# Attention stage: reciprocals spread by broadcast stationary columns, ScalarE's copies of whole turned tiles, four probability buffers

## The chip, the cores and the metric

The program runs on one core of a Trainium2 chip. The metric is the device time of one execution in microseconds (us). The engines are TensorE (PE; its weight loads are listed as PEld), VectorE (DVE), ScalarE (ACT), GpSimd (POOL) and SyncE (SP), which issues DMAs. Each engine works through its own instructions in program order; they meet only at semaphores.

## The reference, cut to what matters

The whole function is two layers of a transformer-like block (attention, a feed-forward with low-rank updates, a fake-quantised product, a mixing of streams with 50 Sinkhorn iterations). The change is in the attention of layer 0: 2 batches, 512 queries, 1024 keys, 32 heads of 32 columns, four heads sharing the keys and values of one of 8 groups.

```python
query = q @ w_q.T                      # q: layernorm(x), (2, 512, 1024)
key = k @ w_k.T                        # k, v: ctx, (2, 1024, 1024)
value = v @ w_v.T
...
scores = jnp.einsum('bghnd,bgsd->bghns', query, key) / D_HEAD ** 0.5
scores = jnp.where(mask, scores, jnp.finfo(scores.dtype).min)
attention = jax.nn.softmax(scores, axis=-1)
out = jnp.einsum('bghns,bgsd->bghnd', attention, value)
out = out.transpose(0, 3, 1, 2, 4).reshape(b, n, D_MODEL)
return out @ w_out.T
```

## The kernel before, in words

The program has five stages, one after another, each in a block of its own with a barrier behind it: `stage_a` (projections), `stage_b` (attention), `stage_c` (output projection and feed-forward), `stage_d` (quantised product), `stage_e` (streams). All is written out by hand in Bass: every engine has its own program, and semaphores order them. Only `stage_b` is touched.

`stage_b` runs over BG = 16 pairs of batch and group. One pair has STEPS = 16 steps, a step being one tile of 128 queries of one head (4 tiles of queries, 4 heads; `k % 16 = 4 * tile + head`). Two pairs make a BODY of 32 steps: the first body is written out (`first=True`), six run in a loop, the last is written out again. UNIT = 8 steps are two query tiles of all four heads.

For step k the data goes so:

1. PE scores: two matmuls (L568) of 128 queries by 512 keys into `psS[k % 2]`.
2. DVE `mask_min` (L704): adds the mask, writes `Sc[k % 4]` and each query's minimum (the scores are negated).
3. ACT `exponentials` (L652): `Pr[k % 2]` and the row sums in `sums`. It waits for `masked`, and, as the turns of step k-2 read the same buffer, for `turned[1]` of that step.
4. PE turns the 128x1024 probabilities by eight 128x128 transposes (L618) into `psT`: four into half 0, four into half 1. Each half is one PSUM bank, and there is only one of each.
5. ACT `keep` (L660) copies half 0 to `PT`, DVE `keep` (L713) copies half 1. They count `kept[0]` and `kept[1]`. PE's next turns into a half wait for its count.
6. Eight steps later PE weighs (`weigh`, L582): at each step four matmuls, one for each head, with 32 stationary columns `Vs[:, u, kt, :]` in the strip of columns of that head, 256 queries wide, summing over the eight key tiles kt into `psO`.

PE's order in step k is: scores of step k+2; first four turns of step k; the weighing; last four turns of step k. DVE's is: `mask_min` of step k+2, `keep` of step k. ACT's is: exponential of step k+1, `keep` of step k.

The normalisation is done on the output, which has its queries in columns, while the sums have theirs in partitions. For the pair before, in the steps j of the current pair: at j = 0 DVE takes the reciprocals (`rec`, L717); at j = 8 ACT copies the unnormalised output to `Os` (`keep_O`, L670); at j = 10 PE turns the reciprocals, four transposes of 128x4 (`turn_rec`, L592), at j = 12 ACT copies the result, 4x512, to `recT` (`rec_rows`, L664); at j = 13 PE multiplies it by the 0/1 matrix `headsel` (4x128), so that each head's reciprocals stand on its 32 partitions (`spread_rec`, L598); at j = 15 DVE multiplies (`normalise`, L724) and SP stores. After the last pair the same chain runs with no steps around it.

Of the kernel before, what the change touches and what calls it, by code (L numbers as in the profile page):

```python
# [30 lines left out]
P = 128  # L31
# [420 lines left out]
def stage_b(nc, mask, QHd, QLd, KHd, KLd, Vd, AOd, start_early_loads=None):  # L452
# [4 lines left out]
    with ExitStack() as stack:  # L457
        def sb(name, shape, dt=F32):
            return stack.enter_context(nc.sbuf_tensor(name, shape, dt))
# [6 lines left out]
        UNIT = 2 * HPG  # L466
        UQ = 2 * P
        assert UNIT == NK
        ident = sb("b_ident", [P, P])
        headsel = sb("b_headsel", [HPG, P])  # L470
# [6 lines left out]
        Pr = sb("b_Pr", [P, 2, S2])  # L477
# [4 lines left out]
        recT = sb("b_recT", [HPG, S])  # L482
# [8 lines left out]
        selready = sem("b_selready")  # L491
        mask_in = sem("b_mask_in")
        mbias_ready = sem("b_mbias")
        waited = sem("b_waited")
# [10 lines left out]
        rec_turned = sem("b_recturned")  # L505
        recT_ready = sem("b_recT")
        spread = sem("b_spread")
        O_kept = sem("b_Okept")
        AO_ready = sem("b_AO")
        stored = [sem(f"b_stored{u}") for u in range(2)]  # L510
        block = stack.enter_context(nc.Block())
        QKV_DMAS = 9

        def queries(k):
            return slice(k // HPG % 2 * P, (k // HPG % 2 + 1) * P)
# [43 lines left out]
        @block.tensor  # L559
        def _(pe):  # L560
            def score(it, k, very_first=False):

                u, j = divmod(k, STEPS)
                qt, h = divmod(j, HPG)
                if j == 0 and not very_first:
                    pe.wait_ge(qkv_in[u], (it + 1) * (16 * QKV_DMAS))
                for n in range(2):
                    last = pe.matmul(psS[:, k % 2, n * HALF:(n + 1) * HALF], Qs[:, u, h, qt * P:(qt + 1) * P],  # L568
                                     Ks[:, u, n * HALF:(n + 1) * HALF], start=True, stop=True)
                last.then_inc(scored, 1)  # L570

            def weigh(it, k, first=False):

                u, unit, kt = (k // UNIT - 1) // 2 % 2, k // UNIT - 1, k % UNIT
                if kt == 0:
                    pe.wait_ge(kept[0], it * BODY + k)
                    pe.wait_ge(kept[1], it * BODY + k)
                    if unit % 2 == 0 and not first:
                        pe.wait_ge(AO_ready, it * 2 + (u - 1))
                cols = slice(unit % 2 * UQ, (unit % 2 + 1) * UQ)  # L580
                for h in range(HPG):
                    last = pe.matmul(psO[h * DH:(h + 1) * DH, u, cols], Vs[:, u, kt, :], PT[:, unit % 2, kt, h, :],  # L582
                                     start=(kt == 0), stop=(kt == NK - 1))
                if kt == NK - 1:
                    last.then_inc(weighed, 1)

            def turn_rec(bg, u):

                pe.wait_ge(rec_ready, bg + 1)
                pe.wait_ge(O_kept, bg + 1)  # L590
                for qt in range(QT):
                    last = pe.transpose(psO[0:HPG, u, qt * P:(qt + 1) * P], rec[:, u, qt * HPG:(qt + 1) * HPG],  # L592
                                        ident[:])
                last.then_inc(rec_turned, 1)

            def spread_rec(bg, u):
                pe.wait_ge(recT_ready, bg + 1)
                pe.matmul(psO[:, u, :], headsel[:], recT[:], start=True, stop=True).then_inc(spread, 1)  # L598

            def body(it, first=False, last=False):  # L600
                for k in range(BODY):
                    u, j = divmod(k, STEPS)

                    if not (last and k + 2 >= BODY):
                        pe.wait_ge(masked, it * BODY + (k + 1))
                        if k + 2 < BODY:
                            score(it, k + 2)
                        else:
                            score(it + 1, k + 2 - BODY)
                    pe.wait_ge(probs, it * BODY + (k + 1))  # L610
                    for f in range(2):
                        if f == 1 and not (first and k < UNIT):
                            weigh(it, k, first)
                        if not (first and k == 0):
                            pe.wait_ge(kept[f], it * BODY + k)
                        for t in range(NK // 2):
                            kt = f * (NK // 2) + t
                            last_t = pe.transpose(psT[:, f, t, :], Pr[:, k % 2, kt * P:(kt + 1) * P], ident[:])  # L618
                        last_t.then_inc(turned[f], 1)

                    if not (first and u == 0):
                        if j == UNIT + 2:
                            turn_rec(it * 2 + (u - 1), 1 - u)
                        if j == UNIT + 5:
                            spread_rec(it * 2 + (u - 1), 1 - u)

            pe.wait_ge(setup, 2)
            pe.wait_ge(selready, 4)
# [10 lines left out]
            turn_rec(BG - 1, 1)  # L639
            spread_rec(BG - 1, 1)  # L640

        @block.scalar
        def _(act):
            def exponentials(it, k, first=False):

                act.wait_ge(masked, it * BODY + (k + 1))
                if not (first and k < 2):
                    act.wait_ge(turned[1], it * BODY + (k - 1))
                u, j = divmod(k, STEPS)
                if j == 0 and not first:  # L650
                    act.wait_ge(rec_ready, it * 2 + (u - 1))
                act.activation(Pr[:, k % 2, :], Sc[:, k % 4, :], ACT.Exp, bias=mins[:, k % 4:k % 4 + 1], scale=-1.0,  # L652
                               accum_out=sums[:, u, j:j + 1]).then_inc(probs, 1)

            def keep(it, k, first=False):
                act.wait_ge(turned[0], it * BODY + (k + 1))
                if not (first and k < 2 * UNIT):
                    if k % UNIT == 0:
                        act.wait_ge(weighed, it * (BODY // UNIT) + (k // UNIT - 1))
                act.copy(PT[:, (k // UNIT) % 2, 0:NK // 2, k % HPG, queries(k)], psT[:, 0, :, :]).then_inc(kept[0], 1)  # L660

            def rec_rows(bg, u):
                act.wait_ge(rec_turned, bg + 1)
                act.copy(recT[:], psO[0:HPG, u, :]).then_inc(recT_ready, 1)  # L664

            def keep_O(bg, u, first=False):
                act.wait_ge(weighed, (bg + 1) * (STEPS // UNIT))
# [4 lines left out]
            def body(it, first=False, last=False):  # L672
                for k in range(BODY):
# [6 lines left out]
                    if not (first and u == 0):  # L680
                        if j == UNIT:
                            keep_O(it * 2 + (u - 1), 1 - u, first and u == 1)
                        if j == UNIT + 4:
                            rec_rows(it * 2 + (u - 1), 1 - u)

            act.dma_start(mk8[:], mask.rearrange("(t p) k -> p t k", p=P)).then_inc(mask_in, 16)
            exponentials(0, 0, True)
# [2 lines left out]
                body(it)  # L690
            body(BG // 2 - 1, last=True)
            keep_O(BG - 1, 1)
            rec_rows(BG - 1, 1)

        @block.vector
        def _(dve):
# [9 lines left out]
                                         accum_out=mins[:, k % 4:k % 4 + 1]).then_inc(masked, 1)  # L706

            def keep(it, k, first=False):
                dve.wait_ge(turned[1], it * BODY + (k + 1))
                if not (first and k < 2 * UNIT):  # L710
                    if k % UNIT == 0:
# [14 lines left out]
            def body(it, first=False, last=False):  # L726
                for k in range(BODY):
# [6 lines left out]
                    if not (first and u == 0):  # L734
                        if j == 0:
                            reciprocals(it * 2 + (u - 1), 1 - u)
                        if j == UNIT + 7:
                            normalise(it * 2 + (u - 1), 1 - u, None if first else it * 16)

            dve.sem_inc(stored[1], 16)  # L740
# [15 lines left out]
        @block.gpsimd  # L756
        def _(pool):
            identity(pool, ident, setup)
            pool.memset(headsel[:], 1.0).then_inc(selready, 1)
            pool.wait_ge(selready, 1)  # L760
            pool.affine_select(out=headsel[:], in_=headsel[:], compare_op=ALU.is_ge, fill=0.0, base=0,
                               pattern=[[1, P]], channel_multiplier=-DH).then_inc(selready, 1)
            pool.wait_ge(selready, 2)
            pool.affine_select(out=headsel[:], in_=headsel[:], compare_op=ALU.is_ge, fill=0.0, base=DH - 1,
                               pattern=[[-1, P]], channel_multiplier=DH).then_inc(selready, 2)

# [1214 lines left out]
```

## Time and profile before

| | |
|---|---|
| median of 3 runs | 1275.06 us (lowest 1275.0) |
| span of the profiled execution | 1275.0 us |
| mean granted TensorE clock, whole span | 0.920 |
| PE busy | 1074.9 us (84%) |
| DVE busy | 904.2 us (71%) |
| ACT busy | 670.6 us (53%) |
| POOL busy | 131.5 us (10%) |

The span is the time from the first to the last instruction of one execution, which the profile traces; the runs are timed without it. The busy shares are means over all five stages. The attention stage's first scores start at 237 us and its last operation at 801 us, and it is in the windows and the order of events within it that the change has to be judged. A timeline row gives the start, the time for which the engine was busy with it (several instructions of a kind merged, with their number as x4), and in brackets the idle time ahead and what ended it. Successive merged rows of PE overlap at their ends, since a matmul's last columns are still on their way when the next starts; the distance of two starts is what a piece of PE's work takes.

### The profile page before, as it was taken

To read this page: it belongs to the slowest core of one execution; us is meant where nothing else is said; L and a number is where in the kernel's file an instruction comes from. 1 tells how busy PE (TensorE), PEld (TensorE's weight loads), DVE (VectorE), ACT (ScalarE), POOL (GpSimd) and SP (SyncE) were. 2 spreads that over 40 slices of the span, in tenths; PEclk is the share of its full clock that TensorE was granted. 3 is DMA by queue.
4 is the path that set the end of the run, shared out by engine and by line. 5 is a ranking of instruction groups with operands and counts; after the bars stand their busy time and mean duration, and the time that the engine had idled before them with its cause. 6 is when DMAs were issued, how large, how long until landed. Compare 5 with 4: busy or idle time off the path is not lost. (4 is left out here: it accounts for less than half of the span.)

```text
span 1275.0 us, 20748 instructions
## 1 busy us (share of the span) xinstructions
PE 1074.9 (84%) x6960; PEld 748.7 (59%) x6960; DVE 904.2 (71%) x1889; ACT 670.6 (53%) x1146; POOL 131.5 (10%) x107
## 2 busy tenths in 40 slices
PE   4999899499999999999999999689999967622208
PEld 3788777366666666666666666168888833411107
DVE  6445732598888898888888887535534336689998
ACT  3223310488888888888888887423222156543214
POOL 3111300000000000000000000000032045224300
PEclk8999999699999999999999999889999989855559
DMA  4777931952112222222222110563240000000003
GB/s 167 249 268 265 371 125 38 229 168 59 44 47 44 62 62 62 62 62 62 58 62 62 45 30 10 158 214 96 66 149 0 0 1 1 12 1 0 0 0 132
DMA packets 55719, 112.82 MB, mean 88 GB/s; under 512 B 7884, under 2 KB 21324, under 8 KB 55548
## 3 DMA queue, kind: packets, MB, share of 16 engines
q1 hardware_dynamic: 55084, 111.74, 28.6%
q8 instruction: 25, 0.41, 0.1%
q10 hardware_dynamic: 528, 0.52, 0.1%
q14 instruction: 18, 0.15, 0.0%
q0 software_dynamic: 64, 0.00, 0.0%
HBM read 83.99 MB, written 27.26 MB: 87 GB/s over the span
## 5 line engine op out<-in xcount | busy, mean ns | idle before, releaser
L652 ACT ACTIVATE b_Pr<-b_Sc,b_mins 128x1024 f32<-128x1024 f32 x256 | 294.5, 1150 | 94.8 <-PE b_psT L618 70.8
L704 DVE CUSTOM_DVE_ANT_0 b_Sc<-b_psS,b_mbias 128x1024 f32<-128x1024 f32 x256 | 312.3, 1220 | 28.5 <-PE b_psS L568 28.3
L618 PE MATMUL b_psT<-b_ident,b_Pr 128*128 128x128 f32 x2048 | 321.0, 280 | 0.9 <-ACT b_PT L660 0.2
L618 PEld LDWEIGHTS b_psT<-b_ident,b_Pr 128*128 128x128 f32 x2048 | 235.0, 141 | 140.3 <-issue 99.9
L713 DVE COPY b_PT<-b_psT 128x512 f32<-128x512 f32 x256 | 176.9, 691 | 42.6 <-PE b_psT L618 40.1
L568 PE MATMUL b_psS<-b_Ks,b_Qs 128*128 128x512 f32 x512 | 183.1, 439 | 17.5 <-DMA b_Qs<-QLd 14.4
L582 PE MATMUL b_psO<-b_PT,b_Vs 128*32 128x256 f32 x2048 | 162.2, 390 | 1.3 <-DVE b_PT L713 0.9
L660 ACT COPY b_PT<-b_psT 128x512 f32<-128x512 f32 x256 | 145.1, 567 | 13.8 <-PE b_psT L618 13.2
L568 PEld LDWEIGHTS b_psS<-b_Ks,b_Qs 128*128 128x128 f32 x512 | 78.3, 193 | 29.6 <-issue 25.2
L1039 ACT ACTIVATE c_sd<-c_mv,c_eps 128x1 f32<-128x1 f32 x16 | 4.7, 295 | 142.9 <-DVE c_mv L1121 142.9
L270 PE MATMUL a_psM<-XTh,WTh 128*128 128x512 f32 x192 | 75.7, 394 | 3.6 <-DVE WTl L345 3.6
L270 PE MATMUL a_psM<-XTh,WTl 128*128 128x512 f32 x192 | 75.2, 392 | 0.0
L270 PE MATMUL a_psM<-XTl,WTh 128*128 128x512 f32 x192 | 75.2, 392 | 0.0
L1114 DVE TENSOR_TENSOR XR<-XR,c_psM 128x1024 f32 (+1 forms) x16 | 19.5, 1221 | 75.4 <-PE c_psM L950 75.4
L582 PEld LDWEIGHTS b_psO<-b_PT,b_Vs 128*32 128x32 f32 x2048 | 42.0, 108 | 44.6 <-issue 43.7
L314 ACT ACTIVATE a_oh<-a_psM 128x512 fp32r<-128x512 f32 x24 | 14.4, 598 | 98.1 <-PE a_psM L270 91.9
L1615 PE MATMUL e_psT<-e_XN,e_dg 128*128 x128 | 30.0, 399 | 41.2 <-DVE XR L1870 41.2
L381 DVE SCALAR_TENSOR_TENSOR a_ol<-a_psM,a_oh 128x512 fp32r<-128x512 f32 x24 | 16.6, 691 | 64.9 <-ACT a_oh L314 64.9
L60 POOL MEMSET c_ident<- 128x128 f32 x1 | 0.2, 204 | 574.1 <-POOLq L457 574.1
L950 PE MATMUL c_psM<-WOh,c_Lh 128*128 128x512 f32 x128 | 51.8, 405 | 4.2 <-issue 4.2
L1615 PEld LDWEIGHTS e_psT<-e_XN,e_dg 128*128 128x128 f32 x128 | 25.7, 202 | 45.7 <-issue 41.9
L950 PE MATMUL c_psM<-WOh,c_Ll 128*128 128x512 f32 x128 | 51.8, 404 | 0.0
(219 smaller groups left out, 1673.0 us busy)
## 6 DMA issues: line engine op xcount, KB each, us to landing
a_xn<-in_ctx_turned SPq DMA_DIRECT2D x16, 512.0 KB, 3.4
XS<-in_ctx SPq DMA_DIRECT2D x16, 512.0 KB, 5.8
b_Qs<-QHd SPq DMA_DIRECT2D x30, 256.0 KB, 4.6
b_Qs<-QLd SPq DMA_DIRECT2D x30, 256.0 KB, 5.2
XS<-in_x SPq DMA_DIRECT2D x8, 512.0 KB, 10.2
a_wst<-in_L_xattn_w_q SPq DMA_DIRECT2D x8, 512.0 KB, 5.1
Q2d<-a_q SPq DMA_DIRECT2D x16, 256.0 KB, 4.7
QHd<-a_oh SPq DMA_DIRECT2D x16, 256.0 KB, 4.0
```

The lines of the kernel that those rows point to most:

```text
L270: last = pe.matmul(psM[:, slot, :], a[:, w_slot, k, :], m[:, k, cols], start=(k == 0 and a is WTh and m is mh), stop=(k == KT - 1 and a is ...
L381: dve.scalar_tensor_tensor(out=ol[:, slot, :], in0=psM[:, ps_slot, :], scalar=scale, in1=oh[:, slot, :].bitcast(F32), op0=ALU.mult, op1=AL ...
L568: last = pe.matmul(psS[:, k % 2, n * HALF:(n + 1) * HALF], Qs[:, u, h, qt * P:(qt + 1) * P], Ks[:, u, n * HALF:(n + 1) * HALF], start=True ...
L582: last = pe.matmul(psO[h * DH:(h + 1) * DH, u, cols], Vs[:, u, kt, :], PT[:, unit % 2, kt, h, :], start=(kt == 0), stop=(kt == NK - 1))
L618: last_t = pe.transpose(psT[:, f, t, :], Pr[:, k % 2, kt * P:(kt + 1) * P], ident[:])
L652: act.activation(Pr[:, k % 2, :], Sc[:, k % 4, :], ACT.Exp, bias=mins[:, k % 4:k % 4 + 1], scale=-1.0, accum_out=sums[:, u, j:j + 1]).then ...
L660: act.copy(PT[:, (k // UNIT) % 2, 0:NK // 2, k % HPG, queries(k)], psT[:, 0, :, :]).then_inc(kept[0], 1)
L704: dve.tensor_tensor_reduce(out=Sc[:, k % 4, :], in0=psS[:, k % 2, :], in1=mbias[:, qt, :], scale=1.0, scalar=3.4e38, op0=ALU.add, op1=ALU.min,
L713: dve.tensor_copy(PT[:, (k // UNIT) % 2, NK // 2:NK, k % HPG, queries(k)], psT[:, 1, :, :]).then_inc(kept[1], 1)
L950: last = pe.matmul(psM[:, u, cols], a[:, u, k, :], w[:, k, cols], start=(k == 0 and i == 0), stop=(k == KT - 1 and i == 2))
L1114: dve.tensor_tensor(row, row, psM[:, u, :], ALU.add).then_inc(added, 1)
L1615: last = pe.matmul(psX(u)[:, i * CH:(i + 1) * CH], dg[:, u, n, i, :], XN[:, ds(t, 1), n * CH:(n + 1) * CH].rearrange("p a n -> p (a n)"), ...
```

## The change

It does three things in `stage_b`, and nothing elsewhere.

`Pr` has PR = 4 buffers in place of 2. ACT's exponential of step k waits for the turns of step k-4.

In steps j = 2, 7 and 12 of each pair (`WHOLE`), ACT's `keep` copies both halves of `psT` in one instruction of 128x1024, for which it waits for `turned[1]`, and counts `kept[0]`; DVE's `keep` does nothing in these steps. `kept[1]` then counts only the other steps (`HALVED`, `halved(k)`), and PE doesn't wait for it where the step before was a whole one.

The reciprocals aren't turned. `spread_rec` (new L589) does 16 matmuls at j = 10: for each tile of queries and each head, the column of reciprocals, read 32 times over (`to_broadcast`), is the 128x32 stationary operand, and the 128x128 identity moves. The product has in all 32 partitions of the head's strip the reciprocals of the 128 queries. `turn_rec`, `rec_rows`, `headsel` and `recT` go. `normalise` moves from j = 15 to j = 13.

```diff
+        PR = 4
+        WHOLE = (2, 7, 12)
+        HALVED = BODY - 2 * len(WHOLE)
...
+        def halved(k):
+            return sum(i % STEPS not in WHOLE for i in range(k))
...
-            def turn_rec(bg, u):
+            def spread_rec(bg, u):
                 pe.wait_ge(rec_ready, bg + 1)
                 pe.wait_ge(O_kept, bg + 1)
                 for qt in range(QT):
-                    last = pe.transpose(psO[0:HPG, u, qt * P:(qt + 1) * P], rec[:, u, qt * HPG:(qt + 1) * HPG],
-                                        ident[:])
-                last.then_inc(rec_turned, 1)
-            def spread_rec(bg, u):
-                pe.wait_ge(recT_ready, bg + 1)
-                pe.matmul(psO[:, u, :], headsel[:], recT[:], start=True, stop=True).then_inc(spread, 1)
+                    for h in range(HPG):
+                        one = rec[:, u, qt * HPG + h:qt * HPG + h + 1].to_broadcast([P, DH])
+                        last = pe.matmul(psO[h * DH:(h + 1) * DH, u, qt * P:(qt + 1) * P], one, ident[:],
+                                         start=True, stop=True)
+                last.then_inc(spread, 1)
...
                     for f in range(2):
                         if f == 1 and not (first and k < UNIT):
                             weigh(it, k, first)
-                        if not (first and k == 0):
-                            pe.wait_ge(kept[f], it * BODY + k)
+                        if f == 1 and k and (k - 1) % STEPS not in WHOLE:
+                            pe.wait_ge(kept[1], it * HALVED + halved(k))
+                        elif f == 1 and k == 0 and not first:
+                            pe.wait_ge(kept[1], it * HALVED)
+                        elif f == 0 and not (first and k == 0):
+                            pe.wait_ge(kept[0], it * BODY + k)
...
-                if not (first and k < 2):
-                    act.wait_ge(turned[1], it * BODY + (k - 1))
+                if not (first and k < PR):
+                    act.wait_ge(turned[1], it * BODY + (k + 1 - PR))
...
             def keep(it, k, first=False):
-                act.wait_ge(turned[0], it * BODY + (k + 1))
+                whole = k % STEPS in WHOLE
+                act.wait_ge(turned[1 if whole else 0], it * BODY + (k + 1))
                 if not (first and k < 2 * UNIT):
                     if k % UNIT == 0:
                         act.wait_ge(weighed, it * (BODY // UNIT) + (k // UNIT - 1))
-                act.copy(PT[:, (k // UNIT) % 2, 0:NK // 2, k % HPG, queries(k)], psT[:, 0, :, :]).then_inc(kept[0], 1)
+                if whole:
+                    act.copy(PT[:, (k // UNIT) % 2, :, k % HPG, queries(k)],
+                             psT[:].rearrange("p f t n -> p (f t) n")).then_inc(kept[0], 1)
+                else:
+                    act.copy(PT[:, (k // UNIT) % 2, 0:NK // 2, k % HPG, queries(k)], psT[:, 0, :, :]
+                             ).then_inc(kept[0], 1)
...
-                        if j == UNIT + 7:
+                        if j == UNIT + 5:
                             normalise(it * 2 + (u - 1), 1 - u, None if first else it * 16)
```

On PE, before, the turn of the reciprocals at j = 10 and what stands around it (L568 scores, L618 turns of the probabilities, L582 weighing):

```order
L582 MATMUL b_psO<-b_PT,b_Vs 32x256 x4
L618 MATMUL b_psT<-b_ident,b_Pr 128x128 [waits b_kept1]
L618 MATMUL b_psT<-b_ident,b_Pr 128x128 x3
L592 MATMUL b_psO<-b_ident,b_rec 4x128 [waits b_Okept,b_rec]
L592 MATMUL b_psO<-b_ident,b_rec 4x128 x3
L568 MATMUL b_psS<-b_Ks,b_Qs 128x512 [waits b_masked]
L568 MATMUL b_psS<-b_Ks,b_Qs 128x512
L618 MATMUL b_psT<-b_ident,b_Pr 128x128 [waits b_kept0,b_probs]
```

The same place in the changed kernel (its lines L570, L622 and L584 are the scores, turns and weighing):

```order
L584 MATMUL b_psO<-b_PT,b_Vs 32x256 x4
L622 MATMUL b_psT<-b_ident,b_Pr 128x128 [waits b_kept1]
L622 MATMUL b_psT<-b_ident,b_Pr 128x128 x3
L596 MATMUL b_psO<-b_ident,b_rec 32x128 [waits b_Okept,b_rec]
L596 MATMUL b_psO<-b_ident,b_rec 32x128 x15
L570 MATMUL b_psS<-b_Ks,b_Qs 128x512 [waits b_masked]
L570 MATMUL b_psS<-b_Ks,b_Qs 128x512
L622 MATMUL b_psT<-b_ident,b_Pr 128x128 [waits b_kept0,b_probs]
```

Sixteen matmuls stand where four transposes stood, and the matmul `b_psO<-b_recT,b_headsel` with its wait, three steps on, is gone.

On ACT, in the changed kernel, steps 6 to 9 of a pair (L651 exponential, L664 copy of half 0, L661 copy of both halves, L671 output copy):

```order
L651 ACTIVATE b_Pr,b_sums<-b_Sc,b_mins 128x1024 [waits b_turned1,b_masked]
L664 COPY b_PT<-b_psT 128x4x128 [waits b_turned0]
L645 REGISTER_ALU
L651 ACTIVATE b_Pr,b_sums<-b_Sc,b_mins 128x1024 [waits b_turned1,b_masked]
L661 COPY b_PT<-b_psT 128x8x128 [waits b_turned1]
L645 REGISTER_ALU
L651 ACTIVATE b_Pr,b_sums<-b_Sc,b_mins 128x1024 [waits b_turned1,b_masked]
L664 COPY b_PT<-b_psT 128x4x128 [waits b_weighed,b_turned0]
L668 ISA
L670 REGISTER_ALU [waits b_weighed]
L671 COPY b_Os<-b_psO 128x512 [waits b_AO]
```

The order of kinds is as before; the copy of step 7 has become twice as wide and waits for the last turns of its own step, where all copies of the kernel before wait for the first ones.

## Rows read from the trace of the kernel before

**Rows 1.** Windows: busy us of each engine (instructions), granted clock, DMA share, GB/s

```profile
500.00:600.00 100.00, 99.92 (x854) 63.97 (x846) 87.87 (x145) 81.86 (x145) 0.00 (x0) 1.00 0.25 58
```

**Rows 2.** Timeline, a steady step: start us, us, engine, line, out<-in

```profile
663.95 0.71 PE L568 MATMUL b_psS<-b_Ks,b_Qs 128*128 128x512 f32 x2
...
664.50 0.60 PE L618 MATMUL b_psT<-b_ident,b_Pr 128*128 128x128 f32 x4
...
665.03 0.64 PE L582 MATMUL b_psO<-b_PT,b_Vs 128*32 128x256 f32 x8
...
665.45 0.56 ACT L660 COPY b_PT<-b_psT 128x512 f32<-128x512 f32 x1
...
665.60 0.66 PE L618 MATMUL b_psT<-b_ident,b_Pr 128*128 128x128 f32 x4
...
666.01 0.71 PE L568 MATMUL b_psS<-b_Ks,b_Qs 128*128 128x512 f32 x2
...
666.30 0.69 DVE L713 COPY b_PT<-b_psT 128x512 f32<-128x512 f32 x1 [0.18 <-PE b_psT L618]
...
666.36 1.15 ACT L652 ACTIVATE b_Pr<-b_Sc,b_mins 128x1024 f32<-128x1024 f32 x1 [0.35 <-PE b_psT L618]
666.56 0.60 PE L618 MATMUL b_psT<-b_ident,b_Pr 128*128 128x128 f32 x4
```

**Rows 3.** Timeline, the step with the old spread and the next

```profile
649.90 0.66 PE L618 MATMUL b_psT<-b_ident,b_Pr 128*128 128x128 f32 x4
...
651.53 0.73 PE L568 MATMUL b_psS<-b_Ks,b_Qs 128*128 128x512 f32 x2
...
652.11 0.60 PE L618 MATMUL b_psT<-b_ident,b_Pr 128*128 128x128 f32 x4
652.54 1.22 DVE L704 CUSTOM_DVE_ANT_0 b_Sc<-b_psS,b_mbias 128x1024 f32<-128x1024 f32 x1 [1.26 <-PE b_psS L568]
652.63 0.16 PEld L582 LDWEIGHTS b_psO<-b_PT,b_Vs 128*32 128x32 f32 x8 [0.17 <-issue]
652.63 0.64 PE L582 MATMUL b_psO<-b_PT,b_Vs 128*32 128x256 f32 x8
652.74 0.58 ACT L660 COPY b_PT<-b_psT 128x512 f32<-128x512 f32 x1 [0.85 <-PE b_psT L618]
...
653.20 0.66 PE L618 MATMUL b_psT<-b_ident,b_Pr 128*128 128x128 f32 x4
...
653.62 0.71 PE L568 MATMUL b_psS<-b_Ks,b_Qs 128*128 128x512 f32 x2
```

**Rows 4.** The page's costliest groups: busy, mean ns, idle before, releaser

```profile
L652 ACT ACTIVATE b_Pr<-b_Sc,b_mins 128x1024 f32<-128x1024 f32 x256 | 294.5, 1150 | 94.8 <-PE b_psT L618 70.8
```

**Rows 5.** ACT's groups by form, the turned x tiles of stage A

```profile
L298 ACT ACTIVATE XTh<-a_psT 128x1024 fp32r<-128x1024 f32 x8 | 8.1, 1018 | 5.1 <-PE a_psT L262 5.1
```

**Rows 6.** Timeline, among the first eight steps, without weighing

```profile
251.91 0.57 ACT L660 COPY b_PT<-b_psT 128x512 f32<-128x512 f32 x1
...
252.62 1.17 PE L618 MATMUL b_psT<-b_ident,b_Pr 128*128 128x128 f32 x8
```

**Rows 7.** Timeline, the step with the old turn of the reciprocals

```profile
643.28 0.66 PE L618 MATMUL b_psT<-b_ident,b_Pr 128*128 128x128 f32 x4
...
644.13 0.71 PE L568 MATMUL b_psS<-b_Ks,b_Qs 128*128 128x512 f32 x2
```

**Rows 8.** Timeline, the end of the attention stage

```profile
794.57 3.66 PE L582 MATMUL b_psO<-b_PT,b_Vs 128*32 128x256 f32 x64 [0.88 <-DVE b_PT L713]
...
798.29 0.58 ACT L670 COPY b_Os<-b_psO 128x512 f32<-128x512 f32 x1 [5.13 <-PE b_psO L582]
...
801.44 0.69 DVE L724 TENSOR_TENSOR b_AOs<-b_psO,b_Os 128x512 f32<-128x512 f32 x1 [6.26 <-PE b_psO L598]
```

**Rows 9.** Timeline, weight loads of 512-column f32 passes in stage C

```profile
812.38 0.12 PEld L961 LDWEIGHTS c_psM<-XR,c_wf 128*40 128x40 f32 x1 [0.31 <-issue]
812.81 0.12 PEld L961 LDWEIGHTS c_psM<-XR,c_wf 128*40 128x40 f32 x1 [0.31 <-issue]
```

More of the change, by code:

```diff
@@ L468, in stage_b @@
         assert UNIT == NK
+        PR = 4
+        WHOLE = (2, 7, 12)
+        HALVED = BODY - 2 * len(WHOLE)
         ident = sb("b_ident", [P, P])
-        headsel = sb("b_headsel", [HPG, P])
         mk8 = sb("b_mk8", [P, QT, S2], U8)
@@ L476, in stage_b @@
         Sc = sb("b_Sc", [P, 4, S2])
-        Pr = sb("b_Pr", [P, 2, S2])
+        Pr = sb("b_Pr", [P, PR, S2])
         PT = sb("b_PT", [P, 2, NK, HPG, UQ])
@@ L481, in stage_b @@
         rec = sb("b_rec", [P, 2, STEPS])
-        recT = sb("b_recT", [HPG, S])
         Os = sb("b_Os", [P, S])
@@ L490, in stage_b @@
         setup = sem("b_setup")
-        selready = sem("b_selready")
         mask_in = sem("b_mask_in")
@@ L504, in stage_b @@
         rec_ready = sem("b_rec")
-        rec_turned = sem("b_recturned")
-        recT_ready = sem("b_recT")
         spread = sem("b_spread")
@@ L576, in weigh @@
                     pe.wait_ge(kept[0], it * BODY + k)
-                    pe.wait_ge(kept[1], it * BODY + k)
+                    pe.wait_ge(kept[1], it * HALVED + halved(k))
                     if unit % 2 == 0 and not first:
@@ L613, in body @@
                             weigh(it, k, first)
-                        if not (first and k == 0):
-                            pe.wait_ge(kept[f], it * BODY + k)
+                        if f == 1 and k and (k - 1) % STEPS not in WHOLE:
+                            pe.wait_ge(kept[1], it * HALVED + halved(k))
+                        elif f == 1 and k == 0 and not first:
+                            pe.wait_ge(kept[1], it * HALVED)
+                        elif f == 0 and not (first and k == 0):
+                            pe.wait_ge(kept[0], it * BODY + k)
                         for t in range(NK // 2):
                             kt = f * (NK // 2) + t
-                            last_t = pe.transpose(psT[:, f, t, :], Pr[:, k % 2, kt * P:(kt + 1) * P], ident[:])
+                            last_t = pe.transpose(psT[:, f, t, :], Pr[:, k % PR, kt * P:(kt + 1) * P], ident[:])
                         last_t.then_inc(turned[f], 1)
[L621 to L625, printed above, removed]
+                    if j == UNIT + 2 and not (first and u == 0):
+                        spread_rec(it * 2 + (u - 1), 1 - u)
             pe.wait_ge(setup, 2)
-            pe.wait_ge(selready, 4)
             pe.wait_ge(first_in, 16 * 8)
@@ L638, in _ @@
                 weigh(BG // 2, k)
-            turn_rec(BG - 1, 1)
             spread_rec(BG - 1, 1)
@@ L651, in exponentials @@
                     act.wait_ge(rec_ready, it * 2 + (u - 1))
-                act.activation(Pr[:, k % 2, :], Sc[:, k % 4, :], ACT.Exp, bias=mins[:, k % 4:k % 4 + 1], scale=-1.0,
+                act.activation(Pr[:, k % PR, :], Sc[:, k % 4, :], ACT.Exp, bias=mins[:, k % 4:k % 4 + 1], scale=-1.0,
                                accum_out=sums[:, u, j:j + 1]).then_inc(probs, 1)
             def keep(it, k, first=False):
-                act.wait_ge(turned[0], it * BODY + (k + 1))
+                whole = k % STEPS in WHOLE
+                act.wait_ge(turned[1 if whole else 0], it * BODY + (k + 1))
                 if not (first and k < 2 * UNIT):
@@ L659, in keep @@
                         act.wait_ge(weighed, it * (BODY // UNIT) + (k // UNIT - 1))
-                act.copy(PT[:, (k // UNIT) % 2, 0:NK // 2, k % HPG, queries(k)], psT[:, 0, :, :]).then_inc(kept[0], 1)
-            def rec_rows(bg, u):
-                act.wait_ge(rec_turned, bg + 1)
-                act.copy(recT[:], psO[0:HPG, u, :]).then_inc(recT_ready, 1)
+                if whole:
[4 more added lines that the diff above has]
+                             ).then_inc(kept[0], 1)
             def keep_O(bg, u, first=False):
@@ L682, in body @@
                             keep_O(it * 2 + (u - 1), 1 - u, first and u == 1)
-                        if j == UNIT + 4:
-                            rec_rows(it * 2 + (u - 1), 1 - u)
             act.dma_start(mk8[:], mask.rearrange("(t p) k -> p t k", p=P)).then_inc(mask_in, 16)
@@ L692, in _ @@
             keep_O(BG - 1, 1)
-            rec_rows(BG - 1, 1)
         @block.vector
@@ L708, in keep @@
             def keep(it, k, first=False):
+                if k % STEPS in WHOLE:
+                    return
                 dve.wait_ge(turned[1], it * BODY + (k + 1))
@@ L758, in _ @@
             identity(pool, ident, setup)
[L759 to L765, printed above, removed]
 class EarlyLoads:
```

## The prediction

> **What bounds the kernel now.** I read the windows first, to see which engine is full in the attention stage and at what clock; then a steady step in order of time, to see whether PE is full because it works or because it is late; then the places where the step is not steady. The stage runs from about 240 to 802 us of the 1275.0 us span, 256 steps (16 groups of 16). In a window in its middle PE is busy 99.92 of 100 us at granted clock 1.00, that is 2.4 GHz, while DVE has 87.87 and ACT 81.86 us [rows 1]. PE's busy time alone proves little, so take the step apart [rows 2]. PE starts the scores of step k+2 at 663.95, the first four turns of step k at 664.50, the weighing at 665.03, the last four turns at 665.60 and the next scores at 666.01: pieces of 0.55, 0.53, 0.57 and 0.41 us, **2.06 us** in all. What the pieces wait for is long there: ACT's copy of half 0, which the first turns need, ends at 665.45 + 0.56 = 666.01 and PE uses it at 666.56; the exponential for those turns is the one a step ahead of that at 666.36, so it ended at 666.36 + 1.15 - 2.06 = 665.45, 1.1 us early. The test of this is the step after the old spread matmul, where PE had been held for over a microsecond and both evacuating engines had run dry: ACT's copy there waits 0.85 us for PE, DVE's masking 1.26 us. Its pieces are 0.58, 0.52, 0.57 and 0.42 [rows 3], no shorter. So a step of PE's own work is 2.06 us, and ACT and DVE have slack that nobody is waiting for. A change gains here only by taking work from PE, and loses whatever makes PE wait.
>
> **Part 1: four probability buffers.** ACT waits 70.8 us in all for the turns before its exponentials [rows 4], because `Pr[k % 2]` is read by the turns of step k-2. With four buffers that wait goes, and the exponential starts when `masked` allows. But its result is 1.1 us early already [rows 2], so PE gains 0. What is late next on ACT is nothing that PE sees.
>
> **Part 2: the whole copies.** In steps 2, 7 and 12 of 16, DVE's copy of half 1 (it has slack: gain 0) goes to ACT, and ACT's one copy waits for `turned[1]` instead of `turned[0]`. This is a new wait on the path. PE's first turns of step k+1 write half 0 of `psT`, which the whole copy of step k still reads, and they wait for `kept[0]`. Count from the start of the last four turns of step k. In the steady step PE comes to the next first turns after 0.41 + 0.55 = 0.96 us. Now the copy starts when the last turn has landed: DVE's copy shows it, 666.30 - 665.60 = 0.70 us (ACT's exponential, which the same event releases, starts 0.76 us after) [rows 2]. A copy of 128x1024 f32 from PSUM by ACT took 1.018 us in the stage ahead [rows 5]; I take 1.0. From the end of such a copy to the turns that it releases is 252.62 - (251.91 + 0.57) = 0.14 us [rows 6], in the first eight steps, which have no weighing and where that wait does bind. Sum: 0.70 + 1.00 + 0.14 = 1.84 us against 0.96, a **stall of 0.9 us**. Nothing else of PE's queue can fill it: the scores of step k+3 already stand in the 0.96, and behind the held turns are the weighing and the last turns, in order. Bounds: 0.8 (copy and landing at their fastest) and 1.0 (ACT released at 0.76, and another 0.04 to start turns whose weights can't be loaded early).
>
> Does it end there? ACT next has an exponential (1.15) and the half copy (0.57) of step k+1, so `kept[0]` for k+1 comes 1.70 + 1.15 + 0.57 = 3.42 us after my zero, and PE wants it at 1.84 + 2.06 = 3.90: met. At step 7 the output copy of 0.58 (`keep_O`, behind step 8's half copy) and another pair follow: 3.42 + 0.58 + 1.15 + 0.57 = 5.72 plus 0.14 against 3.90 + 2.06 = 5.96: just met. So each whole copy costs its stall and no more. There are 48; the two among the first eight steps come where ACT itself is nearly full (1.15 + 0.57 us a step), so that each costs at least the 0.45 us more that ACT works and at most the stall; I take 0.6 each. 46 x 0.9 + 2 x 0.6 = **+42.6 us** (bounds 46 x 0.8 = 37 and 46 x 1.0 + 1.2 = 47).
>
> **Part 3: the reciprocals.** What goes: the turn of the reciprocals lengthens the last-turns piece from 0.41 to 644.13 - 643.28 = 0.85, 0.44 us [rows 7]; the old spread matmul lengthens it to 651.53 - 649.90 = 1.63, 1.22 us [rows 3]. Together 1.66 us, in 15 of 16 groups. ACT's copy of `recT` goes too, under cover: 0. What comes: 16 matmuls of a 128x32 stationary column by 128 columns of the identity. The weighing's matmuls (4 to a step in the program, 8 in the trace, so two passes each) have the same stationary shape. 
>
> At the very end nothing covers this chain: from the end of the output copy, 798.29 + 0.58 = 798.87, to `normalise` at 801.44 are 2.57 us [rows 8]: turn, ACT copy, spread. In its place stand 0.14 of release, 1.1 and 0.1: -1.2 us. The mask of the spread (`headsel`) is built on POOL while PE waits for its first loads: 0. `normalise` two steps earlier on DVE: the spread is ended two steps before it, and DVE is spared a copy of 0.69 us [rows 2] at step 12: 0.
>
> Do 32 weight loads hide? In the weighing they do: 57 ns a pass leaves nothing for its load [rows 8]. "TensorE: Matmul & The Clock Gate" of the Trainium skill speaks against it: by its section The mechanism a load overlaps matmuls in flight only where the row group differs (here all rows are in use), and by LDWEIGHTS a load of P columns takes P/1.2 ns. An estimate by that page is 32 x 27 ns = 0.85 us more per visit, which makes the sum 1321; the trace agrees with neither for the weighing, and no run here tests passes as short as these.
>
> **Sum**, against the profiled execution: 1275.0 + 42.6 - 8.4 - 1.2 = **1308 us**. Its span is the median of the runs (1275.06), so nothing is added for what lies around it. By its own bounds this case goes from 1275 + 37 - 12 - 1.3 = 1299 to 1275 + 47 - 3.6 - 0.9 = 1318.
>
> **Rivals.** *Weight loads not hidden in the spread.* A pass of 128 columns gives a load half the cover that the weighing gives. The weighing's eight loads take 0.16 us together [rows 3], so 32 take 0.64; if none is hidden the visit is 1.1 + 0.6 = 1.7, the gain per group 0 and at the end 0.6: 1275 + 42.6 - 0.6 = 1317. Against it: in the 64 passes of [rows 8] the loads cost next to nothing.
>
> *Strips one after another*: 3.4 us per visit, 1275 + 42.6 + 26 + 1.1 = 1345. For it: each head now has its own stationary column, where the weighing loads one and the same for four. Against it: the strips are as separate.
>
> *The other side, PE relieved.* From weighing to turns PE takes 0.14 us more than the stream (0.57 - 0.43), and from scores to turns I allow as much. If these were waits on evacuations that the two more buffers and the lighter DVE remove, 208 ordinary steps would gain up to 0.28 each, 58 us: 1308 - 58 = 1250, no longer slower. It offsets the stalls from (42.6 - 9.6) / 208 = 0.16 us a step. [rows 3] speaks against it: the same gaps with both engines idle ahead.
>
> *The whole copy doesn't hold PE* (the stall falls under cover that I don't see): 1275 - 9.6 = 1265. Against it: `psT` has one buffer of each half.
>
> **Chances.** The sum 0.74, loads not hidden 0.09, strips in turn 0.06, PE relieved 0.04, no stall 0.05, some 0.02 for a lower clock in the gaps. The range leaves out the last four: 1293 to 1330. The measurement can tell about 2%, 25.5 us, so "slower" begins at 1300.6: all of the first three but the lowest edge of the sum. Faster by over 2% 0.02 (half of PE relieved), within 2% 0.13, slower 0.85.
>
> **What would show it.** In the profile after: ordinary steps of 2.06 us; at each whole copy a step of 2.96, with PE (or its loads) waiting for ACT's `b_PT`, 48 times, some 40 us; ACT no longer waiting for turns before exponentials, but before whole copies; the visit of the 16 matmuls lengthening its step by 1.1 instead of two by 0.44 and 1.22. The prediction is wrong if ordinary steps get shorter than 2.06, if the whole copy takes other than 1.0 us, or if the visit takes over 2 us.

## The result and the profile after

| | before | after |
|---|---|---|
| median | 1275.03 us (4 runs) | 1310.8 us (1307.33 to 1313.0, 4 runs) |
| span of the profiled execution | 1275.0 us | 1309.0 us |
| first scores of the attention stage | 237.16 us | 236.22 us |
| last `normalise` of it | 801.44 us | 834.41 us |

The ratio is 1.0268, 95% interval 1.0252 to 1.0285: **slower by 2.7%**. The two medians of the table divide to 1.0281, inside this interval. Forecast were 1308 us and a range of 1293 to 1330. One of the runs of before lies at 2187 us and is left out of the ratio. From first scores to last `normalise` the stage takes 598.2 us where it took 564.3, 33.9 more, and the span grew by 34.0: what lies outside the stage changed by 0.1 in sum.

The page's groups of the changed kernel that answer to [rows 4], and the new copy (busy, mean ns | idle before, releaser):

```profile
L622 PE MATMUL b_psT<-b_ident,b_Pr 128*128 128x128 f32 x2048 | 322.2, 281 | 35.5 <-ACT b_PT L661 35.1
...
L651 ACT ACTIVATE b_Pr<-b_Sc,b_mins 128x1024 f32<-128x1024 f32 x256 | 295.1, 1153 | 68.6 <-DVE b_mins L702 66.7
...
L661 ACT COPY b_PT<-b_psT 128x1024 f32<-128x1024 f32 x48 | 48.7, 1014 | 42.2 <-PE b_psT L622 42.0
```

PE's turns now stand idle 35.1 us for ACT's whole copies, 48 of them at 1.014 us. Before they stood idle 0.9 us:

```profile
L618 PE MATMUL b_psT<-b_ident,b_Pr 128*128 128x128 f32 x2048 | 321.0, 280 | 0.9 <-ACT b_PT L660 0.2
```

The 35.1 are 0.73 a copy and less than the stall: the row of the scores ahead of a wait runs to its end at 0.70 us, where the turns of an ordinary step follow after 0.55, and only what is behind that end is listed as idle. ACT's exponentials no longer wait for the turns, as the four buffers intend, but for DVE's minima instead: 68.6 us of idle time where there were 94.8. That ACT waits less there has brought PE nothing.

A whole step in the timeline of the changed kernel, step 7 of a pair; it answers to [rows 2]:

```profile
660.90 0.66 PE L622 MATMUL b_psT<-b_ident,b_Pr 128*128 128x128 f32 x4
...
661.31 0.70 PE L570 MATMUL b_psS<-b_Ks,b_Qs 128*128 128x512 f32 x2
...
661.59 1.01 ACT L661 COPY b_PT<-b_psT 128x1024 f32<-128x1024 f32 x1 [0.95 <-PE b_psT L622]
...
662.75 0.63 PE L622 MATMUL b_psT<-b_ident,b_Pr 128*128 128x128 f32 x4 [0.74 <-ACT b_PT L661]
...
663.31 0.64 PE L584 MATMUL b_psO<-b_PT,b_Vs 128*32 128x256 f32 x8
...
663.88 0.66 PE L622 MATMUL b_psT<-b_ident,b_Pr 128*128 128x128 f32 x4
...
664.29 0.71 PE L570 MATMUL b_psS<-b_Ks,b_Qs 128*128 128x512 f32 x2
...
664.84 0.60 PE L622 MATMUL b_psT<-b_ident,b_Pr 128*128 128x128 f32 x4
...
666.35 0.71 PE L570 MATMUL b_psS<-b_Ks,b_Qs 128*128 128x512 f32 x2
...
666.90 0.60 PE L622 MATMUL b_psT<-b_ident,b_Pr 128*128 128x128 f32 x4
```

Read it along the chain: last turns at 660.90, the copy 0.69 us later (the turns have landed), 1.01 us of it, and 0.15 us after its end at 662.60 the first turns of the next step. From last turns to first turns are 1.85 us where 0.96 would do, a stall of 0.89, and those turns then take 0.56 to the weighing instead of 0.53: 0.92 in all. From scores to scores, 661.31 to 664.29, the step has 2.98 us. In the next step first turns follow scores by 0.55 us (664.84 after 664.29), as always, and so they do in the step behind it, which is the one whose half copy has the output copy ahead of it (666.90 after 666.35): the copy's lateness is gone after one step. Of the 47 whole copies that have scores behind them, 46 give such a step of 2.97 or 2.98 us; the other one, step 2 of the first pair, where there is no weighing yet, gives 2.25.

The visit of the reciprocals, in the same kernel:

```profile
668.00 0.66 PE L622 MATMUL b_psT<-b_ident,b_Pr 128*128 128x128 f32 x4
...
668.59 0.81 PEld L596 LDWEIGHTS b_psO<-b_ident,b_rec 128*32 128x32 f32 x32 [0.17 <-issue]
668.59 1.08 PE L596 MATMUL b_psO<-b_ident,b_rec 128*32 128x128 f32 x32
...
669.60 0.30 PEld L570 LDWEIGHTS b_psS<-b_Ks,b_Qs 128*128 128x128 f32 x2 [0.20 <-issue]
669.60 0.73 PE L570 MATMUL b_psS<-b_Ks,b_Qs 128*128 128x512 f32 x2
```

The last turns' piece has 1.60 us, 1.19 more than its 0.41, in place of 1.66 more by the two old visits [rows 3, 7]. The weight loads take 0.81 us (overlaps counted once) and lie inside the 1.01 us between the starts. At the stage's end the chain from output copy to `normalise` answers to [rows 8]:

```profile
832.55 0.59 ACT L671 COPY b_Os<-b_psO 128x512 f32<-128x512 f32 x1 [5.13 <-PE b_psO L584]
...
833.28 1.08 PE L596 MATMUL b_psO<-b_ident,b_rec 128*32 128x128 f32 x32 [0.79 <-ACT b_Os L671]
834.41 0.69 DVE L724 TENSOR_TENSOR b_AOs<-b_psO,b_Os 128x512 f32<-128x512 f32 x1 [5.57 <-PE b_psO L596]
```

From 833.14 to 834.41 are 1.27 us, where there were 2.57.

### The profile page after: what moved, and what is told of

Read it like the earlier page. It is cut to its first block and busy times, and to the rows that moved or that the text cites. A ratio compares the mean times of both kernels' runs of the same rounds, so it can differ in the third digit from the quotient of the medians.

```text
span 1309.0 us, 21653 instructions
## 1 busy us (share of the span) xinstructions
PE 1077.2 (82%) x7376; PEld 747.7 (57%) x7376; DVE 874.6 (67%) x1841; ACT 683.6 (52%) x1130; POOL 126.4 (10%) x104
## 5 line engine op out<-in xcount | busy, mean ns | idle before, releaser
L622 PE MATMUL b_psT<-b_ident,b_Pr 128*128 128x128 f32 x2048 | 322.2, 281 | 35.5 <-ACT b_PT L661 35.1
L622 PEld LDWEIGHTS b_psT<-b_ident,b_Pr 128*128 128x128 f32 x2048 | 230.6, 141 | 188.0 <-issue 155.0
L651 ACT ACTIVATE b_Pr<-b_Sc,b_mins 128x1024 f32<-128x1024 f32 x256 | 295.1, 1153 | 68.6 <-DVE b_mins L702 66.7
L570 PE MATMUL b_psS<-b_Ks,b_Qs 128*128 128x512 f32 x512 | 182.9, 438 | 17.1 <-DMA b_Qs<-QLd 14.2
L713 DVE COPY b_PT<-b_psT 128x512 f32<-128x512 f32 x208 | 143.8, 691 | 73.8 <-PE b_psT L622 71.6
L584 PE MATMUL b_psO<-b_PT,b_Vs 128*32 128x256 f32 x2048 | 162.1, 391 | 0.9 <-DVE b_PT L713 0.9
L664 ACT COPY b_PT<-b_psT 128x512 f32<-128x512 f32 x208 | 119.5, 574 | 19.2 <-PE b_psT L622 15.8
L570 PEld LDWEIGHTS b_psS<-b_Ks,b_Qs 128*128 128x128 f32 x512 | 78.2, 193 | 21.2 <-issue 17.4
L661 ACT COPY b_PT<-b_psT 128x1024 f32<-128x1024 f32 x48 | 48.7, 1014 | 42.2 <-PE b_psT L622 42.0
L584 PEld LDWEIGHTS b_psO<-b_PT,b_Vs 128*32 128x32 f32 x2048 | 41.5, 108 | 43.5 <-issue 40.7
L943 PE MATMUL c_psM<-WOl,c_Lh 128*128 128x512 f32 x128 | 52.4, 410 | 0.0
```

Of the source, the lines that this page charges most:

```text
L622: last_t = pe.transpose(psT[:, f, t, :], Pr[:, k % PR, kt * P:(kt + 1) * P], ident[:])
L651: act.activation(Pr[:, k % PR, :], Sc[:, k % 4, :], ACT.Exp, bias=mins[:, k % 4:k % 4 + 1], scale=-1.0, accum_out=sums[:, u, j:j + 1]).the ...
L661: act.copy(PT[:, (k // UNIT) % 2, :, k % HPG, queries(k)], psT[:].rearrange("p f t n -> p (f t) n")).then_inc(kept[0], 1)
L713: dve.tensor_copy(PT[:, (k // UNIT) % 2, NK // 2:NK, k % HPG, queries(k)], psT[:, 1, :, :]).then_inc(kept[1], 1)
L943: last = pe.matmul(psM[:, u, cols], a[:, u, k, :], w[:, k, cols], start=(k == 0 and i == 0), stop=(k == KT - 1 and i == 2))
```

## The experiments

Beside the experiments the kernel before has a median of 1276.6 to 1277.0 us, 2 above that of the first comparison, so kernels are compared by their ratio to it. The difference of two such ratios is uncertain by some 4 us. "The stage" is, as above, the time from the first scores to the last `normalise` in a run's trace; it is read to 0.1 us, from one execution each.

**One part at a time.** The changed kernel without whole copies:

```diff
-        WHOLE = (2, 7, 12)
+        WHOLE = ()
```

> The changed kernel without whole copies (no step is one), so four buffers and the new spread alone. My theory: the new visit costs 1.19 us where turn and old spread cost 1.66, 15 times, and the end chain is 1.3 us shorter: 1275 - 7 - 1.3 = 1267 us. Rival, the whole copies are harmless and the visit or the buffers cost the time: about 1310 us.

Measured: 1267.04 us, ratio 0.9925 (0.9901 to 0.9949). The buffers and the new spread alone are a gain of 0.75%, and the whole copies turn it into a loss: 1.0268 - 0.9925 = 0.0343, or 43.7 us, 0.91 for each of 48. The stage takes 556.3 us here, so by the traces the whole copies cost 598.2 - 556.3 = 41.9 us, 0.87 each, and the rest of the change gains 564.3 - 556.3 = 8.0.

The whole copies alone, in the kernel before:

```diff
+        WHOLE = (2, 7, 12)
+        HALVED = BODY - 2 * len(WHOLE)
...
-                act.wait_ge(turned[0], it * BODY + (k + 1))
+                whole = k % STEPS in WHOLE
+                act.wait_ge(turned[1 if whole else 0], it * BODY + (k + 1))
```

(with the copy, the counts and DVE's `keep` as in the change).

> The kernel before with the whole copies of steps 2, 7 and 12 and nothing else of the change (two buffers, old turn and spread). My theory: 46 stalls of 0.92 us and two of 0.6: 1275 + 43.5 = 1318.5 us. Rival, that whole copies need the four buffers to do any good or harm: a different stall, with ACT's exponentials late: above 1325 us, or no stall: 1275 us.

Measured: 1319.14 us, ratio 1.0331 (1.0305 to 1.0356): 42.2 us. The stage grows from 564.3 to 606.2 us, by 41.9, as it does with the rest of the change around it. PE's turns wait 35.1 us for the copy in 48 records, as in the changed kernel. The parts add up: 1.0331 times 0.9925 is 1.0254, the measured one 1.0268 (from 1.0252). The whole copy doesn't need the buffers to do its harm.

Four buffers alone, in the kernel before:

```diff
-        Pr = sb("b_Pr", [P, 2, S2])
+        PR = 4
+        Pr = sb("b_Pr", [P, PR, S2])
...
-                if not (first and k < 2):
-                    act.wait_ge(turned[1], it * BODY + (k - 1))
+                if not (first and k < PR):
+                    act.wait_ge(turned[1], it * BODY + (k + 1 - PR))
```

> The kernel before with four probability buffers and nothing else. My theory: PE never waits for an exponential, so 1275 us, with ACT's 71 us of waits for the turns gone or given to another releaser. Rival, PE relieved: ordinary steps get shorter than 2.06 us, 1217 to 1260 us.

Measured: 1276.41 us, ratio 0.9995 (0.9983 to 1.0007): nothing. Its ordinary steps have 2.05 to 2.07 us. Its waits in the stage (engine, line, waited for, us, times, longest):

```profile
ACT b_Pr L653 <- DVE b_mins L705: 69.8, 176, 0.9
...
ACT b_Pr L653 <- PE b_psT L619: 5.2, 11, 0.6
```

Of the 71 us that ACT had waited for turns, 5 are left and 70 stand now at DVE's minima. A wait of an engine that nobody waits for changed its name. This and the unchanged ordinary steps put an end to the rival in which PE is relieved.

**Is it ACT's work or the late release?** ACT takes both halves in the same steps, but in two instructions, and half 0 is given back at once (`kept[1]` counts every step again, and PE waits for it as before):

```diff
-                whole = k % STEPS in WHOLE
-                act.wait_ge(turned[1 if whole else 0], it * BODY + (k + 1))
+                act.wait_ge(turned[0], it * BODY + (k + 1))
...
+                act.copy(PT[:, (k // UNIT) % 2, 0:NK // 2, k % HPG, queries(k)], psT[:, 0, :, :]).then_inc(kept[0], 1)
+                if k % STEPS in WHOLE:
+                    act.wait_ge(turned[1], it * BODY + (k + 1))
+                    act.copy(PT[:, (k // UNIT) % 2, NK // 2:NK, k % HPG, queries(k)], psT[:, 1, :, :]
+                             ).then_inc(kept[1], 1)
```

> The changed kernel in which ACT still takes both halves in steps 2, 7 and 12, but in two instructions: half 0 as soon as its turns have landed, counted at once, then half 1, counted in kept[1]. ACT has more work than in the changed kernel (two copies of 0.57 for one of 1.01) and DVE the same relief. My theory, the stall is the late release of half 0: it goes, 1267 us, as without whole copies. Rival, the cost is ACT's added work or its place in the chain: 1305 us or more.

Measured: 1270.29 us, ratio 0.9942 (0.9924 to 0.996). ACT has about as much work as in the changed kernel (464.8 us busy in the stage for 468.0, its copies of `psT` added up 174.7 for 168.2) and the ratio is 0.0326 lower. The step in its timeline:

```profile
645.58 0.66 PE L618 MATMUL b_psT<-b_ident,b_Pr 128*128 128x128 f32 x4
...
646.27 0.59 ACT L658 COPY b_PT<-b_psT 128x512 f32<-128x512 f32 x1 [0.48 <-PE b_psT L618]
...
646.53 0.60 PE L618 MATMUL b_psT<-b_ident,b_Pr 128*128 128x128 f32 x4
...
647.89 0.57 ACT L655 COPY b_PT<-b_psT 128x512 f32<-128x512 f32 x1
...
648.04 0.71 PE L570 MATMUL b_psS<-b_Ks,b_Qs 128*128 128x512 f32 x2
...
648.61 0.63 PE L618 MATMUL b_psT<-b_ident,b_Pr 128*128 128x128 f32 x4
```

The copy of half 1 starts at the same 0.69 us after the last turns as the whole copy did, but PE is at the next first turns after 0.95: half 0 has long been given back. So the cost is the release of a buffer held by a wider instruction, and not, but for a small part, ACT's load. That part can be read as well: the stage takes 559.0 us, 2.7 more than without whole copies. ACT's half copy of the step behind ends only at 648.46. The turns that it releases come 0.15 us later, at 648.61, 0.57 after their scores for 0.55, and from these scores to the next are 2.11 us for 2.06. So of the 41.9 us 39.2 are the late release.

**Is the price per copy?** Six whole steps of 16:

```diff
-        WHOLE = (2, 7, 12)
+        WHOLE = (1, 3, 6, 9, 12, 14)
```

> The changed kernel with six whole steps of 16 (1, 3, 6, 9, 12, 14) in place of three. My theory: the stall is paid per whole copy, 48 more of 0.92 us: 1311 + 44 = 1355 us. Rival, ACT's total work decides, which is under a step's time by a margin until some point: a sudden rise or none, below 1330 or above 1370 us.

Measured: 1354.06 us, ratio 1.0599 (1.0574 to 1.0625). The 48 further copies cost 0.0331, 42 us, 0.88 each; by the stage, 642.6 us, it is 44.4, 0.92 each. It is a price per copy, with no threshold up to six in 16 steps.

**Can PE's own queue fill the stall?** In the steps behind steps 2 and 12 the weighing goes ahead of the first turns:

```diff
+                    early = k > 0 and (k - 1) % STEPS in WHOLE and k % UNIT != 0
                     for f in range(2):
-                        if f == 1 and not (first and k < UNIT):
+                        if f == (0 if early else 1) and not (first and k < UNIT):
                             weigh(it, k, first)
```

> The changed kernel with PE's weighing put ahead of the first turns in the steps behind steps 2 and 12 (behind step 7 it needs that step's copy and stays). My theory: 0.57 us of the stall of 0.92 is then covered in 32 of 48 places, less what is lost to the other order: 1310.8 - 32 x 0.53 = 1294 us. Rival, PE was held by something else than the first turns' wait: no change, 1311 us.

Measured: 1298.13 us, ratio 1.0166 (1.014 to 1.0193), 13 us less than the changed kernel, of 17 expected. Its timeline:

```profile
642.40 0.70 PE L570 MATMUL b_psS<-b_Ks,b_Qs 128*128 128x512 f32 x2
...
643.03 0.64 PE L584 MATMUL b_psO<-b_PT,b_Vs 128*32 128x256 f32 x8
...
643.75 1.09 PE L623 MATMUL b_psT<-b_ident,b_Pr 128*128 128x128 f32 x8
...
644.60 0.71 PE L570 MATMUL b_psS<-b_Ks,b_Qs 128*128 128x512 f32 x2
644.74 0.58 ACT L665 COPY b_PT<-b_psT 128x512 f32<-128x512 f32 x1
...
645.46 0.63 PE L623 MATMUL b_psT<-b_ident,b_Pr 128*128 128x128 f32 x4
```

The step itself falls from 2.98 to 2.20 us, almost an ordinary one. But ACT, which has still done the whole copy, an exponential and only then the half copy, ends that at 645.32, and the next first turns come 0.86 us after the scores where 0.55 is usual. (The trace puts their wait down to the exponential, but that had ended at 644.74.) The step in which they stand has 2.40 us for 2.05, so that the two steps together have 4.59 for 5.03, 0.44 less: the stall had been ACT's time to catch up. The first eight steps have no weighing that could go ahead, so there are 31 such places and not the 32 of my expectation: 13.6 us. The stage is 13.8 shorter, 584.4 us.

**The visit, by itself.** Without whole copies, every matmul of the visit done twice:

```diff
-                for qt in range(QT):
-                    for h in range(HPG):
+                for again in range(2):
+                    for qt in range(QT):
+                        for h in range(HPG):
```

> The kernel without whole copies, with all 16 matmuls of the visit done twice (the same values again). It prices the visit without its opening. If loads are hidden and strips work side by side, 32 more passes cost 0.86 us in 16 visits: 1267 + 14 = 1281 us. If part of the loads is exposed, 1.5 us or more each: from 1291 us. With strips in turn 3.4 us each: 1321 us.

Measured: 1283.6 us, ratio 1.0047 (1.0031 to 1.0064), 0.0122 or 15.6 us above the kernel without the second half, 0.97 a visit; by the stage, 570.2 us, it is 13.8, 0.87 a visit, as in its timeline:

```profile
612.03 1.95 PE L597 MATMUL b_psO<-b_ident,b_rec 128*32 128x128 f32 x64
613.91 0.73 PE L570 MATMUL b_psS<-b_Ks,b_Qs 128*128 128x512 f32 x2
```

The same 16 matmuls, head by head instead of tile by tile:

```diff
-                for qt in range(QT):
-                    for h in range(HPG):
+                for h in range(HPG):
+                    for qt in range(QT):
```

> The kernel without whole copies, with the 16 matmuls in another order: the four query tiles of one head, then the next head, so that neighbours use the same strip of columns. If the strips are side by side only when neighbouring matmuls name different strips, the visit takes 32 x 0.107 = 3.4 us, 2.4 more: 1267 + 37 = 1304 us. If each strip has a queue of its own, nothing changes: 1267 us.

Measured: 1289.48 us, ratio 1.0098 (1.0073 to 1.0123), 22 us above; the stage is 22.1 longer.

```profile
616.45 2.46 PE L596 MATMUL b_psO<-b_ident,b_rec 128*32 128x128 f32 x32
618.84 0.73 PE L570 MATMUL b_psS<-b_Ks,b_Qs 128*128 128x512 f32 x2
```

The visit has 2.39 us, 75 ns a pass, neither the 27 of separate queues nor the 107 of one after another. Neither expectation was right. The order of the loops is worth 1.4 us a visit; why it isn't the full factor of four was not tried.

**Less going in and out.** Without whole copies, two key tiles are weighed in every second step:

```diff
-                        if f == 1 and not (first and k < UNIT):
-                            weigh(it, k, first)
+                        if f == 1 and k % 2 == 0 and not (first and k < UNIT):
+                            for more in range(2):
+                                weigh(it, k + more, first)
```

> The kernel without whole copies, in which PE weighs two key tiles in every second step instead of one in each. The same matmuls, half as many changes between turns and weighing. My theory, each change in and out costs 0.14 to 0.24 us of PE's own time, and with no weighing ahead of them the last turns of the odd step wait some 0.14 us for DVE's copy: 124 pairs save 0.1 to 0.23, so 1267 - 18 = 1249 us (1239 to 1256). Rival, the single psT then binds through the copies, and the gain is eaten: 1264 us or more.

Measured: 1259.53 us, ratio 0.9866 (0.984 to 0.9891), the fastest of all kernels here, 0.0059 or 7.5 us below the one without pairs (7.9 by the stage). It fell between the two expectations. A quiet pair of steps and the start of the next:

```profile
619.61 0.71 PE L570 MATMUL b_psS<-b_Ks,b_Qs 128*128 128x512 f32 x2
...
623.54 0.70 PE L570 MATMUL b_psS<-b_Ks,b_Qs 128*128 128x512 f32 x2
...
625.62 0.69 DVE L714 COPY b_PT<-b_psT 128x512 f32<-128x512 f32 x1
...
626.40 1.07 PE L584 MATMUL b_psO<-b_PT,b_Vs 128*32 128x256 f32 x16 [0.27 <-issue]
...
627.81 0.70 PE L570 MATMUL b_psS<-b_Ks,b_Qs 128*128 128x512 f32 x2
```

The first pair takes 3.93 us instead of two steps' 4.12: 0.19 less, within the 0.1 to 0.23 that I had expected. The second takes 4.27: it begins a new unit, whose weighing needs DVE's copy of the step just before (625.62 + 0.69 = 626.31, weighing at 626.40), and that step had no weighing to cover it.

With four key tiles in every fourth step (2 becomes 4 in the lines above):

> The same with four key tiles in every fourth step. Three steps in a row are then without weighing, where PE would take 1.4 us and DVE, with masking and its copy, takes 1.74. My theory: what three more changes save is lost to waits for the copies, 1270 us (1260 to 1290). Rival, the buffers carry the engines over: as much again as with pairs, 1235 to 1240 us.

Measured: 1294.59 us, ratio 1.0139 (1.0122 to 1.0156), far from my 1270 and outside its bounds of 1260 to 1290; the rival's 1235 to 1240 is further off still. Its longest waits of PE and its loads in the stage for another engine (the rows of PE and PEld in part cover the same time):

```profile
PEld b_psT L623 <- DVE b_PT L714: 42.5, 92, 0.7
PEld b_psT L623 <- ACT b_Pr L652: 30.9, 59, 0.7
PE b_psT L623 <- DVE b_PT L714: 21.2, 74, 0.5
```

So PE waits for DVE's copies and for ACT's results in the steps without weighing. That the slack of the fourth step isn't carried over because `psT` has one buffer a half is my reading; no run tried two.

## Why the prediction was right, point by point

*PE bounds, with 2.06 us of its own a step.* Shown: four buffers alone changed nothing, and ordinary steps are as before.

*The whole copy costs a stall of 0.9 us.* Each term of the sum can be read after: landing 0.70 forecast and 0.69 found, copy 1.00 and 1.01, release 0.14 and 0.15, stall and slower first turns 0.92 together. 43 us were forecast for the 48; by taking them away they are 43.7, by adding them alone 42.2, and 41.9 both ways in the traces' stages. That the cause is the held half of `psT` and not ACT's work is shown by the two-instruction copy, which leaves 2.7 of them.

*It ends there.* Shown for step 7 by the timeline. The prediction had it "just met" there, by 0.1 us; the half copy behind the output copy ends at 666.33 and its turns start at 666.90, so there were 0.4 to spare. The weighing put ahead shows that the room has an end: with 0.78 us taken from the stall ACT is late in the next step.

*The two whole copies among the first eight steps cost 0.6 each, 0.45 at least.* Together they cost 0.85 and not 1.2. Step 2's makes its step 0.51 longer than without whole copies (2.25 us for 1.74), but the two steps behind it are 0.24 shorter, so it costs 0.27, under the least that I allowed; step 7's costs 0.58 (2.98 for 2.40).

*The visit costs 1.1.* It costs 1.19 (1.01 between the starts and 0.18 ahead of it), so a group gains 0.47 and not 0.56, 1.4 us less over the run than in the sum. The stream was right, 0.87 for 0.86; the price for going in and out was mis-sized, 0.32 where the prediction had 0.14 and rounded up to 0.24. The rivals of exposed loads and of strips in turn are gone by the 27 ns a pass. The estimate from the Trainium skill ("TensorE: Matmul & The Clock Gate", The mechanism and LDWEIGHTS), 0.85 us more for 32 loads over full rows, doesn't hold: doing all 32 once more cost 0.87 us altogether. The same section also lets a load go ahead where it targets the background weight buffer, which the prediction left out; hidden loads agree with that, but no run here shows by which way they were hidden.

*End chain -1.2.* Found: 1.27 for 2.57, -1.3.

*Where the 3 us between 1308 and 1310.8 are.* In the traces the stage grew by 33.9 us where the sum has 33.0. The whole copies make 41.9 of it for 42.6, and the rest of the change gives back 8.0 for 9.6, mostly by the visit. That the 42.6 came so close is in part luck: the 46 full stalls are 0.92 and not 0.90 (0.9 us more), the two early ones 0.4 us less, and the remaining 1.2 less are waits of 0.04 to 0.14 us at the start of a unit (steps of 2.10 and 2.20 us without whole copies) that fall into the stalls or are gone beside them, which the prediction didn't consider. The other 2 us are no cost of the change. The changed kernel's profiled run took 1310.84 us with a span of 1309.0, and the kernel before shows the same distance beside the experiments (1276.92 us with 1275.2), but its median in the first comparison, on which the sum was built, is 1275.03, at the span itself. Why that figure lacks the distance is not known. Against the 1276.6 to 1277.0 of the experiments the changed kernel is 34 us longer, as the spans say.

## What to carry to other kernels

When one engine's evacuation is moved to another in a wider instruction, look at when its source buffers come free: a single buffer that was given back in halves is now given back late and whole, and the producer pays landing, the full copy and the release, less what it has to do meanwhile. Two instructions on the same engine in the same steps cost this kernel 2.7 us where the wide one cost 41.9. Deeper buffers ahead of an engine whose results are early only rename its wait.

Small matmuls on separate column strips wanted neighbours on different strips here, and what they cost beyond the stream was the change in and out. Gathering them in pairs gained 7.5 us; by fours the waits for the evacuating engines ate more than that.

## What I had not expected of the hardware

The order of matmuls among the four column strips: the same 32 passes of 128 columns with 128x32 weights took 1.01 us with the strips in rotation and 2.39 us with four matmuls on one strip after another. And with the strips in rotation a weight load for every 27 ns of streaming, 128 rows by 32 columns each, stayed hidden.
